# A long convolution whose last transform writes two 64-column tiles of the array in one pass, fed by gathers that write eight partitions each

## The chip, the core and the metric

The kernel runs on one core of a Trainium2 chip. The metric is the time of one execution on the device, in microseconds (us). One program computes a two-layer decoder for two sequences of 2048 positions and 512 channels; the change touches one of its stages.

## What is computed

The stage in question is the sequence mixing of the second layer. Cut to what matters, with u the normalised input, seen as 4 sequences of 1024 positions:

```python
k = einsum('blh,dh->bdl', u, Wk) + bk ;  v = einsum('blh,dh->bdl', u, Wv) + bv
k = irfft(rfft(k_kernel, n=2*L) * rfft(k, n=2*L))[..., :L] + k_D * k      # first convolution
kv = k * v
y = irfft(rfft(kv, n=2*L) * rfft(ssm_kernel, n=2*L))[..., :L] + kv * D     # second convolution
```

Every channel is convolved on its own with a kernel as long as the sequence. The reference sees 2048 positions per batch entry, so a segment of 1024 positions needs its own part and a part from the segment before it.

## The kernel before

**Stages.** `build_decoder` runs attention, cross attention, feed-forward, projection (`stage_project`, which writes `conv_k`, `conv_v`), the convolution (`stage_conv`, lines 2456 to 2806), the gated output, a second cross attention, routing and 64 experts, one after another. `open_conv` (2429) allocates the tables of the convolution and starts their loads during the projection.

**Steps and slots of the convolution.** The 512 channels are done in two halves of 256 (`hh`). For each half and each of the two convolutions (`conv` 0 and 1) there is one step for the kernel's own transform (a *hat* step, `is_seg` false) and four *segment* steps for (batch b, segment s), s = 0 and 1. That makes 20 steps, n = 0 to 19: hats are n = 0, 5, 10, 15; segments with conv 0 are n = 1 to 4 and 11 to 14, with conv 1 n = 6 to 9 and 16 to 19; in each group of four, s is 0, 1, 0, 1. Each step has four slots q = 0 to 3. What TensorE does in slot (n, q) is written out by hand at lines 2798 to 2806: `back` (inverse transform, 32x64 tiles of the array, line 2788) of the slot before, then the slot's auxiliary units, then `spectrum` (forward transform, 64x32 tiles, line 2775) of the next slot. Auxiliary units are, in q = 0 and 1, four *split* units each of step n+1 (line 2753); in q = 2 and 3, two *join* units each of step n-1 if that was a segment (line 2761). All matmuls are float32 with 512 or 256 columns moving; the trace shows each matmul of the program as two records.

**A join unit** multiplies the gathered `vt` with the table `join`: two matmuls of 128 rows by 128 columns of weights, 512 columns moving, the second accumulated on the first, into one of two banks. The result is multiplied on VectorE into `vb` in conv 0 (`take`, line 2723) or copied on ScalarE in conv 1 (line 2647). A bank is free for unit a+2 when unit a was taken.

**The other engines.** ScalarE copies the split units to `g1` (2645), the spectra of hats (2660) and of segments with s = 0 (2667), and the result of `back` to `v1` (2675). VectorE does the complex product of a segment (`point`): with s = 1 two additions (2699, 2700), then four products (2707) and two sums (2711, 2713); `back` waits for the sums.

**Transfers.** `spread` on the SP queue moves `g1` to `gt` (16 DMAs of 128 KB per step, line 2602, 16 source partitions each). `gather` on the POOL queue moves `v1` to `vt` (16 DMAs of 128 KB per segment step, line 2575): 128 source partitions, and 16 destination partitions, every eighth from `PLACE[r]` on, with 8 KB in each. The same SP queue loads `xin` (2586) and `vb` (2592) and stores `y_out` (2607), 1 MB each over 128 partitions. In steps of conv 0 there is mostly one load of `xin` and one of `vb`; in steps of conv 1 one store. SP issues in the order of lines 2609 to 2624; a split unit's copy to `g1` waits until the `spread` of the step before has landed (2644).

## Time and profile before

| | us |
|---|---|
| median of 3 runs | 5086.95 |
| lowest, highest | 5080.97, 5093.71 |
| profiled execution: time, span | 5107.29, 5105.5 |
| convolution stage in that execution (first to last slot) | 484.3, from 2157.7 to 2642.0 |
| mean granted TensorE clock, whole span | 0.978 of full speed |

The span is the time between the first and last instruction; 1.8 us lie around it. Times in rows are microseconds from the start of the span unless they are called ns. PE is TensorE's matmul, PEld its weight load, DVE VectorE, ACT ScalarE, POOL GpSimd, SP the sync engine; "SPq" and "POOLq" are the instructions by which they issue transfers. An entry such as `[2.63 <-DVE cv_y L2713]` says how long the engine had been idle before the row and what ended that. The DMA share is the mean busy share of the core's 16 DMA engines, counted by their packets, and can be a little over 1.

### The profile page before, as it was taken

The page shows a single profiled execution, that of the slowest core. Times are in us where ns is not written, and L with a number is a line of the kernel's source. Part 1 is how long each engine was busy: PE and PEld are TensorE (multiplying, and loading weights), DVE is VectorE, ACT ScalarE, POOL GpSimd, SP SyncE. Part 2 cuts the span into 40 slices and gives each one's busy share as a digit, 9 for nine tenths or more (in the row PEclk, how much of TensorE's full clock was granted, in tenths as well). Part 3 has the DMA queues.
Part 4 walks back from the last instruction along what each step waited for, and adds up shares of the span by engine and source line. Part 5 has one row for each costly group of instructions (what it writes and reads, how often), then busy time and mean ns, then how long its engine had stood idle before and what let it go on. Part 6 is the DMA issues. An engine that isn't in the chain of part 4 may idle for free. (4 is left out here: it accounts for less than half of the span.)

```text
span 5105.5 us, 124764 instructions
## 1 busy us (share of the span) xinstructions
PE 4847.5 (95%) x49200; PEld 3357.9 (66%) x49200; DVE 2858.2 (56%) x4880; ACT 1662.8 (33%) x2033; POOL 1812.5 (36%) x1684
## 2 busy tenths in 40 slices
PE   9999999989999999989979999789999999999998
PEld 4444445658887756534334566478889888888788
DVE  4244236766654345466752576566666666666665
ACT  1001005544333210045431444233333333333333
POOL 1001004645554411022232234444445444444443
PEclk9999999989999999999989999899999999999999
DMA  1000011141111233397866111146666677889996
GB/s 61 9 33 25 9 58 56 59 117 41 41 34 34 75 109 107 119 245 221 216 210 256 49 51 51 50 118 222 222 221 223 222 248 258 306 304 318 312 316 201
DMA packets 422050, 743.99 MB, mean 146 GB/s; under 512 B 119905, under 2 KB 203622, under 8 KB 415284
## 3 DMA queue, kind: packets, MB, share of 16 engines
q1 hardware_dynamic: 293376, 661.44, 36.9%
q0 software_dynamic: 48448, 76.66, 6.7%
q10 hardware_dynamic: 79988, 2.67, 1.0%
q8 instruction: 155, 2.54, 0.2%
q14 instruction: 83, 0.68, 0.0%
HBM read 559.39 MB, written 107.88 MB: 131 GB/s over the span
## 5 line engine op out<-in xcount | busy, mean ns | idle before, releaser
L3562 PE MATMUL ex_ps<-ex_w,ex_xT 128*32 128x256 f32 x20992 | 1228.3, 380 | 31.4 <-DVE ex_w L3463 22.3
L3562 PEld LDWEIGHTS ex_ps<-ex_w,ex_xT 128*32 128x32 f32 x20992 | 1027.9, 110 | 178.1 <-DVE ex_w L3463 30.7
L3463 DVE COPY ex_w<-ex_shelf 128x4096 f32 x328 | 748.8, 2283 | 329.2 <-PE ex_ps L3562 161.2
L3520 ACT ACTIVATE ex_w<-ex_shelf 128x4096 f32 x164 | 595.0, 3628 | 809.5 <-PE ex_ps L3574 687.8
L3574 PE MATMUL ex_ps<-ex_w,ex_hT 128*32 128x256 f32 x10496 | 650.3, 379 | 9.1 <-ACT ex_w L3520 4.1
L3426 POOL DMA_INDIRECT out<-ex_y,ex_ix_out x164 | 306.6, 1869 | 824.4 <-DVE ex_xT L3450 350.4
L3409 POOL DMA_INDIRECT ex_x<-moe_xn,ex_ix x328 | 528.6, 1612 | 137.4 <-issue 99.1
L3574 PEld LDWEIGHTS ex_ps<-ex_w,ex_hT 128*32 128x32 f32 x10496 | 521.9, 110 | 83.8 <-issue 17.9
L2575 POOL DMA_DIRECT2D cv_vt<-cv_v x256 | 134.1, 530 | 376.6 <-ACT cv_v L2675 372.3
L634 PE MATMUL at_ps<-at_xT,at_kT 128*128 128x512 f32 (+3 forms) x640 | 239.3, 529 | 1.6 <-ACT at_kT L528 1.6
L634 PEld LDWEIGHTS at_ps<-at_xT,at_kT 128*128 128x128 f32 x640 | 116.7, 190 | 121.8 <-issue 109.1
L3525 ACT ACTIVATE ex_g<-ex_ps 128x512 f32<-128x512 f32 x164 | 98.2, 599 | 302.5 <-issue 296.6
L3469 DVE TENSOR_TENSOR ex_h<-ex_g,ex_ps 128x512 f32<-128x512 f32 x164 | 112.3, 685 | 132.3 <-PE ex_ps L3562 78.3
L1880 ACT ACTIVATE ff_gT<-ff_ps,ff_bet,ff_gam 128x128 f32<-128x128 f32 x384 | 137.8, 484 | 121.8 <-PE ff_ps L1923 121.8
L1864 ACT ACTIVATE ff_y<-ff_y,ff_nm,ff_rs 128x512 f32<-128x512 f32 x96 | 72.9, 808 | 268.6 <-POOL ff_nm L1580 268.6
L928 POOL TENSOR_TENSOR xb_s<-xb_s,xb_rec 128x616 f32<-128x616 f32 x64 | 78.0, 1219 | 215.4 <-DVE xb_rec L1002 215.1
L3450 DVE STREAM_TRANSPOSE ex_xT<-ex_x 128x256 f32<-128x256 f32 x164 | 72.5, 442 | 139.6 <-DMA ex_x<-moe_xn,ex_ix 139.4
L592 PE MATMUL at_ps<-at_v,at_low 128*128 128x512 f32 x336 | 146.8, 592 | 0.0
L489 DVE TENSOR_TENSOR at_ps<-at_ps,at_tri 128x128 f32<-128x128 f32 x32 | 9.5, 298 | 234.9 <-PE at_ps L634 234.9
L2322 PE MATMUL pr_ps<-pr_t,pr_s 128*128 128x384 f32 x384 | 135.8, 487 | 1.6 <-DVE pr_t L2245 1.1
L2707 DVE TENSOR_TENSOR cv_m<-cv_z,cv_hat 128x512 f32<-128x512 f32 x128 | 79.9, 686 | 99.9 <-ACT cv_z L2667 99.3
L462 DVE TENSOR_TENSOR at_acc<-at_acc,at_ps 128x512 f32<-128x512 f32 x80 | 54.4, 687 | 135.1 <-PE at_ps L592 135.1
(367 smaller groups left out, 8065.9 us busy)
## 6 DMA issues: line engine op xcount, KB each, us to landing
ex_shelf<-L_ffn_w SPq DMA_DIRECT2D x128, 2048.0 KB
ex_shelf<-L_ffn_wo SPq DMA_DIRECT2D x64, 2048.0 KB
cv_gt<-cv_g SPq DMA_DIRECT2D x320, 128.0 KB
cv_vt<-cv_v POOLq DMA_DIRECT2D x256, 128.0 KB, 3.3
ff_x<-x SPq DMA_DIRECT2D x16, 1024.0 KB
ex_raw_x<-slot_token ACTq DMA_DIRECT2D x656, 0.5 KB
at_low<-x SPq DMA_DIRECT2D x8, 1024.0 KB
x<-at_acc SPq DMA_DIRECT2D x8, 1024.0 KB, 4.2
```

The lines of the kernel that those rows point to most:

```text
L592: i = pe.matmul(ps[:, 4 + n % 4, :], prob[g][:, j % 4, (it - 4 * g) * P:(it - 4 * g + 1) * P], v[:, j, :], start=j == js[0], stop=j == js[-1])
L634: i = pe.matmul(ps[:, bank + ic - origin // CH, lo - ic * CH:], kT[:, k, j * P:(j + 1) * P], xT[:, k, lo:(ic + 1) * CH], start=k == 0, sto ...
L1880: i = act.activation(gT[:, k, j * P:(j + 1) * P], ps[:, side_bank(("g", s, j)), k * P:(k + 1) * P], ACT.Gelu, bias=bet[:, b, k:k + 1], sca ...
L2322: i = pe.matmul(bank[:, 0:NPC], lhs[:, k], rhs[:, k], start=first and k == 0, stop=k == HK - 1, skip_group_check=not first)
L2575: eng.dma_start(vt[PLACE[r]:P:UN, e % 2, q // 2], v1[:, q % 2, a, :]).then_inc(vt_in[e % 2][q], 16)
L3409: pool.indirect_dma_start(out=x[:, p, h, :], out_offset=None, in_=xn_q, in_offset=bass.IndirectOffsetOnAxis(ap=ix[:, p, h:h + 1], axis=0)) ...
L3426: pool.indirect_dma_start(out=out_q, out_offset=bass.IndirectOffsetOnAxis(ap=ix_out[:, p:p + 1], axis=0), in_=y[:, p, :], in_offset=None, ...
L3463: dve.tensor_copy(w_s[n][:, :], pick(shelf[n], buf)).then_inc(w_set[n].sem, 1)
L3469: dve.tensor_tensor(h[:, p % 2], g[:, p % 2], ps[:, 1, :], ALU.mult).then_inc(h_done.sem, 1)
L3520: act.activation(w_s[2][:, :], pick(shelf[2], buf), ACT.Copy).then_inc(w_set[2].sem, 1)
L3562: mm = pe.matmul(ps[r * LANES:(r + 1) * LANES, which, hh * FL:(hh + 1) * FL], xT[:, p % 2, k, hh * LANES:(hh + 1) * LANES], wu[which][:, k ...
L3574: mm = pe.matmul(ps[r * LANES:(r + 1) * LANES, 4, 0:DQ], hT[:, p % 2, k, hh, :], wd[:, k, q * DQ:(q + 1) * DQ], start=k == 0, stop=k == FC ...
```

## The change

The join takes one pass in place of two accumulated ones. Each of its two matmuls now has 64 columns of weights, a full contraction over 128 rows, and writes one half of the bank's partitions. For this every gather brings both halves of its rows (`l` = 0 and 1) into the same partitions, so the gathers write 8 partitions (32 a + q + 4 x) with 16 KB in each instead of 16 partitions with 8 KB. The rows of the data are permuted accordingly: loads and the store are split in two DMAs of 64 partitions each, with new counts in their waits. The tables keep their sizes; `join` has only its first 64 columns in use.

```diff
+def base_row(r):
+    return 32 * (r % 4) + r // 4
...
 def half_rows(v, hh, first=0):
     at = hh * (v.shape[0] // (D // CW)) + first
-    return v[at:at + UN * P, :].rearrange("(p i) d -> p i d", i=UN)
+    return v[at:at + UN * P, :].rearrange("(j l k i) d -> l j k (i d)", l=2, k=2, i=UN)
...
     def early(sp):
-        sp.dma_start(st.xin[:, 0], half_rows(kkT, 0)).then_inc(st.x_in[0], 16)
+        for l in range(2):
+            sp.dma_start(st.xin[64 * l:64 * l + 64, 0], half_rows(kkT, 0)[l]).then_inc(st.x_in[0], 16)
...
         def gather(eng, n, q):
             for a in range(4):
-                r = 4 * (q % 2) + a
-                eng.dma_start(vt[PLACE[r]:P:UN, e % 2, q // 2], v1[:, q % 2, a, :]).then_inc(vt_in[e % 2][q], 16)
+                eng.dma_start(vt[base_row(4 * q + a):base_row(4 * q + a) + 29:4, e % 2], v1[:, q % 2, a, :]).then_inc(vt_in[e % 2][q], 16)
...
-                sp.dma_start(xin[:, l % 2], src).then_inc(x_in[l % 2], 16)
+                for k in range(2):
+                    sp.dma_start(xin[64 * k:64 * k + 64, l % 2], src[k]).then_inc(x_in[l % 2], 16)
...
-                sp.dma_start(vb[:, slot_of[n]], seg_rows(v_in, n)).then_inc(v_in_s[slot_of[n]], 16)
+                for k in range(2):
+                    sp.dma_start(vb[64 * k:64 * k + 64, slot_of[n]], seg_rows(v_in, n)[k]).then_inc(v_in_s[slot_of[n]], 16)
...
-                sp.dma_start(seg_rows(y_out, n), vb[:, slot_of[n]]).then_inc(stored[slot_of[n]], 16)
+                for k in range(2):
+                    sp.dma_start(seg_rows(y_out, n)[k], vb[64 * k:64 * k + 64, slot_of[n]]).then_inc(stored[slot_of[n]], 16)
...
-                    for q in range(2):
-                        rows = vt[:, e % 2, q, 2 * u:2 * u + 2, :].rearrange("p i d -> p (i d)")
-                        i = pe.matmul(bank, join[:, q, :], rows, start=q == 0, stop=q == 1)
+                    for l in range(2):
+                        rows = vt[:, e % 2, l, 2 * u:2 * u + 2, :].rearrange("p i d -> p (i d)")
+                        i = pe.matmul(ps[64 * l:64 * l + 64, a % 2, :], join[:, 0, 0:64], rows, start=True, stop=True)
```

## Rows read from the trace of the kernel before

**Rows 1.** Windows: us, each engine's busy time (instructions), clock, DMA share, GB/s; whole stage.

```profile
2157.70:2642.00 484.30, 435.83 (x5184) 181.12 (x5184) 297.96 (x483) 229.07 (x352) 134.08 (x256) 0.95 0.78 214
```

**Rows 2.** Windows: steps 1 to 4, 5, 6 to 9, 11 to 14, 16 to 19.

```profile
2188.90:2288.00 99.10, 88.96 (x1104) 37.39 (x1104) 74.54 (x122) 42.29 (x63) 31.39 (x60) 0.95 0.95 257
2288.00:2307.90 19.90, 19.90 (x193) 7.96 (x192) 4.26 (x7) 9.97 (x17) 2.38 (x5) 1.00 0.75 188
2307.90:2397.70 89.80, 86.74 (x1105) 36.43 (x1104) 69.94 (x114) 49.26 (x74) 31.06 (x60) 0.96 0.75 207
2417.60:2512.20 94.60, 85.89 (x1112) 36.21 (x1114) 74.56 (x122) 42.91 (x64) 31.14 (x60) 0.98 0.90 257
2532.00:2620.00 88.00, 79.86 (x1094) 33.79 (x1094) 69.92 (x113) 45.01 (x67) 31.34 (x60) 0.96 0.65 184
```

**Rows 3.** Groups of the stage: line, tile, shape, count, busy us, mean ns, idle before.

```profile
L2761 PE MATMUL cv_ps<-cv_vt,cv_join 128*128 128x512 f32 x256 | 120.2, 614 | 6.0 <-DMA cv_vt<-cv_v 6.0
...
L2575 POOL DMA_DIRECT2D cv_vt<-cv_v x256 | 134.1, 530 | 376.6 <-ACT cv_v L2675 372.3 <-issue 4.2
```

**Rows 4.** Timeline, PE: a slot with joins in step 7 (start, us, instruction).

```profile
2346.01 1.09 PE L2775 MATMUL cv_ps<-cv_gt,cv_fwd 64*32 64x256 f32 x32
...
2348.09 3.70 PE L2761 MATMUL cv_ps<-cv_vt,cv_join 128*128 128x512 f32 x8
...
2351.72 1.09 PE L2775 MATMUL cv_ps<-cv_gt,cv_fwd 64*32 64x256 f32 x32
```

**Rows 5.** Page, costliest groups: matmuls of the experts on four 32-column tiles.

```profile
L3562 PE MATMUL ex_ps<-ex_w,ex_xT 128*32 128x256 f32 x20992 | 1228.3, 380 | 31.4 <-DVE ex_w L3463 22.3
```

**Rows 6.** Timeline, PE: two slots in a row that VectorE paces, step 19.

```profile
2604.07 2.01 PE L2788 MATMUL cv_ps<-cv_y,cv_inv 32*64 32x256 f32 x32 [2.63 <-DVE cv_y L2713]
...
2609.00 1.12 PE L2788 MATMUL cv_ps<-cv_y,cv_inv 32*64 32x256 f32 x32 [1.22 <-DVE cv_y L2713]
```

**Rows 7.** Timeline, DVE and ACT: join slots of step 2, first slot of step 3; one ACT copy.

```profile
2235.02 1.28 DVE L2723 TENSOR_TENSOR cv_vb<-cv_ps,cv_vb 128x512 f32<-128x512 f32 x2
2236.22 0.68 DVE L2699 TENSOR_TENSOR cv_zp<-cv_ps,cv_z 128x512 f32<-128x512 f32 x1
...
2241.15 1.28 DVE L2723 TENSOR_TENSOR cv_vb<-cv_ps,cv_vb 128x512 f32<-128x512 f32 x2
2242.61 2.50 DVE L2707 TENSOR_TENSOR cv_m<-cv_z,cv_hat 128x512 f32<-128x512 f32 x4 [0.18 <-ACT cv_z L2667]
...
2245.62 0.68 DVE L2713 TENSOR_TENSOR cv_y<-cv_m 128x512 f32<-128x512 f32 x1
...
2352.92 1.08 ACT L2667 ACTIVATE cv_z<-cv_ps 128x512 f32<-128x512 f32 x2 [0.49 <-PE cv_ps L2775]
```

**Rows 8.** Timeline, PE: join slots of hat step 5, and the tail.

```profile
2299.62 3.70 PE L2761 MATMUL cv_ps<-cv_vt,cv_join 128*128 128x512 f32 x8
...
2304.28 3.70 PE L2761 MATMUL cv_ps<-cv_vt,cv_join 128*128 128x512 f32 x8
...
2627.11 9.21 PE L2761 MATMUL cv_ps<-cv_vt,cv_join 128*128 128x512 f32 x16 [6.02 <-DMA cv_vt<-cv_v]
```

**Rows 9.** Windows: feed-forward weights to 128, then to 32 partitions; loads of xin, vb.

```profile
1041.00:1045.00 4.00, 4.00 (x33) 1.93 (x32) 0.64 (x1) 0.73 (x2) 0.00 (x0) 1.00 1.01 372
1045.50:1049.50 4.00, 3.81 (x48) 3.02 (x46) 3.53 (x7) 2.79 (x4) 2.44 (x2) 1.00 1.01 195
2195.00:2199.00 4.00, 3.99 (x39) 1.84 (x40) 2.98 (x5) 3.17 (x5) 1.02 (x2) 1.00 1.05 354
```

**Rows 10.** DMA queues, 2185 to 2630: packets, MB, share of the engines; POOL's queue.

```profile
q0 software_dynamic: 12288, 33.57, 27.6%
```

**Rows 11.** Timeline, SP: the issues of one step's spread.

```profile
2246.88 12.58 SPq L2602 DMA_DIRECT2D cv_gt<-cv_g  x16
```

**Rows 12.** Timeline, PE: the end of a stall in step 2.

```profile
2225.40 3.54 PE L2753 MATMUL cv_ps<-cv_xin,cv_split 128*128 128x512 f32 x4 [3.89 <-ACT cv_g L2645]
```

**Rows 13.** Windows: the stretch of that stall.

```profile
2222.00:2227.00 5.00, 1.60 (x2) 0.84 (x3) 1.68 (x3) 2.00 (x3) 1.55 (x3) 0.82 1.09 246
```

More of the change, by code:

```diff
@@ L2416, in transform_tables @@
     by_row = np.arange(P).reshape(UN, P // UN)[np.argsort(PLACE)].T.reshape(P)
-    split = split.reshape(P, 2, P)[:, :, by_row]
-    join = join.reshape(2, P, P)[:, by_row]
+    halved = np.arange(P).reshape(RES, 2, 2).transpose(1, 0, 2).reshape(P)
+    by_slot = np.array([[base_row(r) + 4 * x for x in range(UN)] for r in range(RES // 2)]).reshape(P)
+    split = split.reshape(P, 2, P)[halved][:, :, by_row]
+    narrow = np.zeros((RES, 2, 2, RES, 2))
+    for k in range(2):
+        narrow[:, :, k, :, k] = join[:, :, 0, :, 0]
+    join = np.zeros((2, P, P))
+    join[0, by_slot, 0:P // 2] = narrow.reshape(P, P // 2)
+    inv = inv.reshape(4, RT, RES // 8, 2, 2, 2, 2, 2, UN).swapaxes(6, 7)
     return (split.reshape(P, 2 * P).astype(f), fwd.reshape(P, RES * RT).astype(f),
@@ L2447, in early @@
         sp.dma_start(st.fwd.rearrange("p a b c -> p (a b c)"), tables_d[1]).then_inc(st.tab_in[1], 16)
-        sp.dma_start(st.xin[:, 1], half_rows(k_in, 0)).then_inc(st.x_in[1], 16)
+        for l in range(2):
+            sp.dma_start(st.xin[64 * l:64 * l + 64, 1], half_rows(k_in, 0)[l]).then_inc(st.x_in[1], 16)
         sp.dma_start(st.inv.rearrange("p a b c d -> p (a b c d)"), tables_d[2]).then_inc(st.tab_in[2], 16)
@@ L2606, in store @@
                 st.plain(sp)
-                sp.dma_start(seg_rows(y_out, n), vb[:, slot_of[n]]).then_inc(stored[slot_of[n]], 16)
+                for k in range(2):
+                    sp.dma_start(seg_rows(y_out, n)[k], vb[64 * k:64 * k + 64, slot_of[n]]).then_inc(stored[slot_of[n]], 16)
             spread(0, 0)
@@ L2623, in _ @@
             for p in range(SEGS):
-                sp.wait_ge(stored[p], 16 * NH)
+                sp.wait_ge(stored[p], 32 * NH)
         @block.gpsimd
@@ L2683, in tap @@
                 l = load_of[n]
-                dve.wait_ge(x_in[l % 2], 16 * (l // 2 + 1))
+                dve.wait_ge(x_in[l % 2], 32 * (l // 2 + 1))
                 dve.tensor_tensor(xin[0:1, l % 2, 0, :], xin[0:1, l % 2, 0, :], gain[0:1, hh, conv, :], ALU.add).then_inc(tapped, 1)
@@ L2720, in take @@
                 if u == 0:
-                    dve.wait_ge(v_in_s[slot_of[n]], 16 * (half_of[n] + 1))
+                    dve.wait_ge(v_in_s[slot_of[n]], 32 * (half_of[n] + 1))
                 o = vb[:, slot_of[n], 2 * u:2 * u + 2, :].rearrange("p i d -> p (i d)")
@@ L2747, in aux @@
                         elif n in load_of:
-                            pe.wait_ge(x_in[load_of[n] % 2], 16 * (load_of[n] // 2 + 1))
+                            pe.wait_ge(x_in[load_of[n] % 2], 32 * (load_of[n] // 2 + 1))
                         else:
@@ L2758, in aux @@
                             pe.wait_ge(vt_in[e % 2][q], 64 * (e // 2 + 1))
-                    for q in range(2):
-                        rows = vt[:, e % 2, q, 2 * u:2 * u + 2, :].rearrange("p i d -> p (i d)")
-                        i = pe.matmul(bank, join[:, q, :], rows, start=q == 0, stop=q == 1)
+                    for l in range(2):
+                        rows = vt[:, e % 2, l, 2 * u:2 * u + 2, :].rearrange("p i d -> p (i d)")
+                        i = pe.matmul(ps[64 * l:64 * l + 64, a % 2, :], join[:, 0, 0:64], rows, start=True, stop=True)
                 i.then_inc(aux_mm, 1)
```

2 lines of the change are left out of this document (1 added, 1 removed).

## The prediction

> **What bounds the kernel now.** Only `stage_conv` changes, so I first cut that stage out of the span: 484 us, in which PE is busy 436, VectorE 298, ScalarE 229 and the DMA engines 0.78 of the time [rows 1]. Then the same view by groups of steps, because the stage has two kinds of them [rows 2]. In steps 6 to 9 and 16 to 19 (conv 1) the DMA share is 0.75 and 0.65 and PE is the busiest. In steps 1 to 4 and 11 to 14 (conv 0) PE leads as well, but the DMA engines stand at 0.95 and 0.90: there a second bound lies right behind the first. Third, the groups by line say how much PE time the change touches: 256 records of the join, 120.2 us [rows 3]. Fourth, the timeline of PE shows a join slot without gaps: from one spectrum to the next 5.71 us, of which the join takes 2351.72 - 2348.09 = 3.63 [rows 4]. So PE sets the pace of a join slot, and I have to find for each slot what comes next.
>
> **What one pass saves on PE.** There are 16 segment steps with two join slots each, 32 slots. The four matmuls of a slot stay four, but two can run side by side. No row shows two tiles of 64 columns. The nearest is the experts' group: four tiles of 32 columns, full contraction, 256 columns moving, 1228.3 us / 20992 = 58.5 ns a record [rows 5]. A join record moves 512 columns in 3.63 / 8 = 454 ns [rows 4], so 227 ns for 256 on one tile: four tiles give 3.9 times the throughput. I take 1.85 for two: 3.63 becomes 1.96, a saving of 1.67 per slot, 53 us over 32. The bounds are 0 (no overlap) and 1.82 (exactly half). Slots already change between tile shapes before and after the join, so that adds nothing: 32x64 before, 64x32 after.
>
> **Who is late next, slot by slot.** Two slots now take 11.42 us, and 3.34 less would be 8.08.
> - Segment with s = 1, conv 1 (steps 7, 9, 17, 19): `back` waits for VectorE's sums. Where nothing else held it, VectorE's pitch was 2609.00 - 2604.07 = 4.93 [rows 6]. Two slots: 9.86, with a hand-over of 0.1 about 10.0, so 1.4 saved. Four times: 5.6.
> - s = 0, conv 1 (8, 18): ScalarE's copy of the spectrum (1.08) and VectorE's 2245.62 + 0.68 - 2242.61 = 3.7 follow each other [rows 7]. The first slot's sums are done 5.0 after its spectrum, the second's 3.8 later, then `back` can start: 9.2, against 11.4 now. 2.2 saved, twice: 4.4.
> - s = 1, conv 0 (2, 4, 12, 14): VectorE also takes the join units. Its pitch is 2241.15 - 2235.02 = 6.13 [rows 7], above today's 5.71; the lag is today made good in the next step. Two sums are ready 11.1 after the first spectrum, `back` starts at 11.4 today: 0.2 saved, so nothing.
> - s = 0, conv 0 (3, 13): 3.7 + 1.2 for the units. 1.2 saved, twice: 2.4.
> - Hats (5, 10, 15): no VectorE work but the units; two joins of 3.63 stand in a row with one spectrum each [rows 8]. 3.3 saved, three times: 10.0.
> - Tail: 9.21 us of joins, the first part at half clock, after a wait of 6.02 for the last gather [rows 8]. I take 3 saved.
>
> This makes 25.4, not 53: half of PE's gain is given back to VectorE. Without the 2.4 in conv 0 it is 23.0.
>
> **What the transfers cost.** Gathers: same bytes, same number of issues; POOL's 256 issues of 530 ns are 134 us of a stage of 484 [rows 3] and hide. With destination partitions of 16 KB the packets can only get easier. Now 33.57 MB take 27.6% of 445 us, 123 us [rows 10]; at the 354 GB/s of the loads [rows 9] it would be 95. So 0 to 28 us less DMA time over 16 steps, 0 to 14 over the eight of conv 0; I take 7. Loads and store: 1 MB over 128 partitions becomes twice 512 KB over 64. The rows show what fewer partitions do: at the same full share the feed-forward weights ran at 372 GB/s to 128 partitions and at 195 to 32 (with some smaller pieces among them) [rows 9]. Half the rate would make a 1 MB load 5.6 us in place of 3.0 (1049 KB / 354), +2.6. Conv 0 has two such loads in each of eight steps: 0 to +42 us of DMA time. Free DMA time there is 0.05 x 99.1 + 0.10 x 94.6 = 14.5 [rows 2]. I take +30 for the loads, nearer to the row than to nothing, since the POOL queue can use an engine while the other waits: 30 - 7 - 14.5 = +8.5 us on the eight steps, which also swallows the 2.4 above. In conv 1 one store per step meets a share of 0.65 to 0.75 and hides. SP issues 16 gathers in 12.58 of some 23 us [rows 11]; two or three more issues of about 0.8 fit. The last store ends the stage: one more issue and at most 2.6 for the halves, +1.5. The first loads of `xin` run during the projection, long before their use.
>
> The Trainium skill (SBUF — State Buffer, "Can I just issue two DMAs to hit both halves?") says that 64 partitions reach no more DMA ports than 32, and that two DMAs on the two halves serialise. The row of 195 against 372 agrees for 32; no row shows 64. By that rule alone the load price would be the full +42.
>
> **Sum.** 23.0 - 1.5 - 8.5 = 13 us less. The profiled execution took 5107.3 and would take 5094.3; that execution is 20 us (0.4%) above the median of the runs, so I put the same 13 us on 5086.95: **5074**.
>
> **The rivals.**
> - *The loads cost nothing* (the two halves interleave, or the gathers' relief pays): conv 0 gives 2.4 and pays nothing, 25.4 - 1.5 = 24: 5063. For it: packets of both queues already share the engines up to 1.09 [rows 13]. Against it: the row at half rate. With relief also ending the stalls, 5057.
> - *Slower: the DMA engines become the bound of conv 0.* Place: steps 1 to 4 and 11 to 14. Price: the full 42 us, no relief, 14.5 absorbed, +27.5. It then meets what happens today once: a copy to `g1` waited for a spread, PE stood 3.89 us [rows 12], and the granted clock averaged 0.82 in the window around it [rows 13], that is, part of it at 1.2 GHz. Two or three more such stalls cost 4 to 8. Total -21.5 + 27.5 + 6 = +12: 5099. It decides from a load price of about 36 us on.
> - *Each gather runs on eight of the 16 engines.* If always the same eight, their gather time doubles, 123 us more over the stage (7.7 a step [rows 10]); conv 0 would then lose some 50 us net: 5110 and more. If they alternate, nothing changes. The Trainium skill (DMA: Bandwidth & Descriptors, on why the semaphore goes up by 16) says that the number of engines divides the outermost dimension of both sides, here 8, and that transfers issued from GpSimd take turns among the engines. No row shows it.
> - *The two tiles don't overlap.* Then the join keeps 3.63 and only the transfers count: 0 to +10, 5087 to 5097. The experts' row speaks against it.
>
> **How the numbers follow.** A measurement of this kernel tells about 0.3%, 15 us, from no change. Forecast (loads partly paid, 5066 to 5084): 0.45. Loads free: 0.32. DMA-bound conv 0: 0.15. Same eight engines: 0.03. No overlap: 0.05. Faster by over 0.3% (below 5071.7): all of "loads free" and a quarter of the forecast, 0.43. Slower by over 0.3% (above 5102): 0.12, from the ends of the second, third and fourth rival. Within: 0.45. The range of 8 in 10 leaves out the better end of "free" and the worse half of the slow ones: 5057 to 5099.
>
> **What would show it.** Join slots: the join's records 128x64, two side by side, some 2.0 us a slot; if 3.6, the first step fails. Pitch of PE in join slots 4.9 to 5.1 with idle time before line 2788 put down to `cv_y`: the VectorE step holds. Hat join slots near 3.0. Steps 6 to 10 and 16 to 19 shorter by about 1.4 to 2.2, hats by 3.3. Steps 1 to 4 and 11 to 14 as long as now or longer, DMA share near 1.0, at fewer GB/s while `xin` and `vb` load: the load price. If these steps get shorter, the price was wrong; if conv 1 gets longer too, it is the gathers. The granted clock of conv 0 falling below 0.95 would be the second rival's mark.

## The result

The changed kernel takes 5143.45 us (median of 4 runs, 5135.74 to 5149.74) against 5086.25 (4 runs, 5080.97 to 5093.71): 1.1% slower, ratio 1.011 with an interval of 1.009 to 1.013, 57 us. The forecast was 13 us less, in a range that ended at 5099. Medians and ratios leave out one slow execution, of e11 below (9285 us at a mean granted clock of 0.82, where the others took some 5093).

The profiled execution of the changed kernel took 5135.74 us (span 5133.9, mean granted clock 0.970). The two profiled executions lie only 28 us apart, because before's was 20 us above its median and after's 8 below. So from here on I compare the stage, cut the same way in every kernel: from the start of the first split matmul to the start of the last join matmul. Before it is 2157.7 to 2635.7, 478.0 us; after 2156.1 to 2682.4, **526.3 us**: 48.3 us longer. The other 9 of the 57 us are not located: each stage is that of one execution. To see where the 48.3 lie, I cut it in four at the first copy to `hat` of steps 0, 5, 10 and 15. Quarters 1 and 3 hold the conv 0 segments, quarters 2 and 4 those of conv 1. Columns are those of [rows 1]. Windows of before at these cuts (not among its rows above):

```profile
2174.20:2289.20 115.00, 102.33 (x1256) 42.59 (x1264) 75.74 (x124) 51.31 (x79) 31.68 (x60) 0.94 0.93 251
2289.20:2398.90 109.70, 106.64 (x1304) 44.38 (x1311) 73.57 (x119) 59.83 (x92) 33.44 (x64) 0.97 0.75 204
2398.90:2513.30 114.40, 105.69 (x1304) 44.12 (x1311) 75.66 (x124) 54.68 (x84) 33.44 (x64) 0.99 0.90 253
2513.30:2635.70 122.40, 108.24 (x1295) 45.46 (x1296) 72.99 (x118) 57.88 (x88) 35.52 (x68) 0.94 0.61 170
```

The same windows of the changed kernel:

```profile
2172.60:2308.70 136.10, 97.44 (x1248) 38.31 (x1248) 73.44 (x120) 51.33 (x80) 34.77 (x59) 0.86 1.00 206
2308.70:2419.30 110.60, 92.57 (x1296) 36.73 (x1296) 74.45 (x122) 58.88 (x92) 37.80 (x65) 0.98 0.88 195
2419.30:2557.30 138.00, 101.89 (x1296) 39.14 (x1296) 74.61 (x122) 54.16 (x85) 37.94 (x65) 0.88 0.99 219
2557.30:2682.40 125.10, 95.25 (x1296) 36.82 (x1296) 75.19 (x122) 57.10 (x88) 41.32 (x70) 0.88 0.75 169
```

The quarters of conv 0 are 21.1 and 23.6 us longer, at a full DMA share that moves fewer bytes a second (206 in place of 251 GB/s). The quarters of conv 1 gain nothing either, though PE is busy 13 to 14 us less in each.

The step on PE came as predicted. Timeline of PE, two join slots of step 7 (answering to [rows 4]) and two of the first conv 0 block:

```profile
2366.34 1.12 PE L2804 MATMUL cv_ps<-cv_y,cv_inv 32*64 32x256 f32 x32 [1.25 <-DVE cv_y L2729]
2367.39 1.94 PE L2777 MATMUL cv_ps<-cv_vt,cv_join 128*64 128x512 f32 x8
2369.26 1.09 PE L2791 MATMUL cv_ps<-cv_gt,cv_fwd 64*32 64x256 f32 x32
2371.28 1.12 PE L2804 MATMUL cv_ps<-cv_y,cv_inv 32*64 32x256 f32 x32 [0.92 <-DVE cv_y L2729]
...
2304.58 1.12 PE L2804 MATMUL cv_ps<-cv_y,cv_inv 32*64 32x256 f32 x32 [1.27 <-DVE cv_y L2729]
...
2310.71 1.12 PE L2804 MATMUL cv_ps<-cv_y,cv_inv 32*64 32x256 f32 x32 [2.12 <-DVE cv_y L2729]
```

The join's eight records take 2369.26 - 2367.39 = 1.87 us where they took 3.63, and `back` then comes at VectorE's pitch, 4.94 and 6.13, just the two numbers taken from [rows 6, 7].

What replaced the gain is a wait for gathers. First the groups of the stage (busy, mean ns, idle before), then ScalarE and PE around 2230 us:

```profile
L2777 PE MATMUL cv_ps<-cv_vt,cv_join 128*64 128x512 f32 x256 | 67.9, 655 | 23.0 <-DMA cv_vt<-cv_v 23.0
L2691 ACT ACTIVATE cv_v<-cv_ps 128x1024 f32<-128x1024 f32 x64 | 65.6, 1024 | 173.6 <-DMA cv_vt<-cv_v 99.1 <-PE cv_ps L2804 74.5
```

```profile
2229.44 1.02 ACT L2691 ACTIVATE cv_v<-cv_ps 128x1024 f32<-128x1024 f32 x1 [8.81 <-DMA cv_vt<-cv_v]
2230.36 1.08 ACT L2661 ACTIVATE cv_g<-cv_ps 128x512 f32<-128x512 f32 x2
```

```profile
2231.01 3.39 PE L2769 MATMUL cv_ps<-cv_xin,cv_split 128*128 128x512 f32 x4 [7.02 <-ACT cv_g L2661]
```

Read them upwards. PE stood 7.02 us before a split, because its bank had not been emptied: that is the work of ScalarE's copy to `g1` at 2230.36. That copy stood behind the copy to `v1` at 2229.44, and this one waited 8.81 us for the gathers out of the `v1` buffer it wanted to overwrite. PE's next four split records then took 3.39 us, mostly at the clock's lower level, 1.2 GHz (mean granted clock 0.58 from 2231.0 to 2234.4); four of the same shape take 1.98 at 2349.03. Before, ScalarE waited for gathers 22.7 us in all (7 times); now 99.1 us (21 times). The DMA view of the stage shows the same, before and then after: the queues with packets, MB and share of the engines, and the gathers' issues with the median us to landing.

```profile
q0 software_dynamic: 12288, 33.57, 25.7%
cv_vt<-cv_v POOLq DMA_DIRECT2D x256, 128.0 KB, 3.3
```

```profile
q1 hardware_dynamic: 50080, 68.18, 59.3%
q0 software_dynamic: 20480, 33.70, 29.6%
cv_vt<-cv_v POOLq DMA_DIRECT2D x256, 128.0 KB, 5.3
```

Where q0 held the engines for 25.7% of 478.0 us, 123 us, it now holds them 29.6% of 526.3, 156 us, for the same data. It has 8192 more packets in the stage, 32 for each of the 256 gathers; only 0.13 MB are in them. POOL needs 600 ns for an issue where it needed 530 [rows 3].

### The profile page after: what moved, and what is told of

Read it like the earlier page. It is cut to its first block and busy times, and to the rows that moved or that the text cites. A ratio compares the mean times of both kernels' runs of the same rounds, so it can differ in the third digit from the quotient of the medians.

```text
span 5133.9 us, 124792 instructions
## 1 busy us (share of the span) xinstructions
PE 4789.1 (93%) x49200; PEld 2841.0 (55%) x49200; DVE 2860.4 (56%) x4880; ACT 1659.7 (32%) x2033; POOL 1851.6 (36%) x1684
## 3 DMA queue, kind: packets, MB, share of 16 engines
q1 hardware_dynamic: 293824, 661.44, 38.1%
## 5 line engine op out<-in xcount | busy, mean ns | idle before, releaser
L3578 PE MATMUL ex_ps<-ex_w,ex_xT 128*32 128x256 f32 x20992 | 1173.9, 381 | 35.9 <-DVE ex_w L3479 32.0
L3578 PEld LDWEIGHTS ex_ps<-ex_w,ex_xT 128*32 128x32 f32 x20992 | 683.4, 110 | 498.6 <-DVE ex_w L3479 47.7
L3590 PE MATMUL ex_ps<-ex_w,ex_hT 128*32 128x256 f32 x10496 | 598.3, 380 | 3.9 <-ACT ex_w L3536 3.9
L3442 POOL DMA_INDIRECT out<-ex_y,ex_ix_out x164 | 318.0, 1939 | 782.3 <-DVE ex_xT L3466 284.2
L3590 PEld LDWEIGHTS ex_ps<-ex_w,ex_hT 128*32 128x32 f32 x10496 | 342.9, 110 | 229.6 <-ACT ex_w L3536 5.1
L2588 POOL DMA_DIRECT2D cv_vt<-cv_v x256 | 151.8, 600 | 408.5 <-ACT cv_v L2691 380.0
L634 PEld LDWEIGHTS at_ps<-at_xT,at_kT 128*128 128x128 f32 x640 | 116.7, 190 | 121.8 <-issue 109.1
L3466 DVE STREAM_TRANSPOSE ex_xT<-ex_x 128x256 f32<-128x256 f32 x164 | 72.7, 443 | 157.9 <-DMA ex_x<-moe_xn,ex_ix 157.9
L2769 PE MATMUL cv_ps<-cv_xin,cv_split 128*128 128x512 f32 x192 | 109.7, 714 | 45.6 <-ACT cv_g L2661 36.1
```

Source lines behind the costliest of these rows:

```text
L634: i = pe.matmul(ps[:, bank + ic - origin // CH, lo - ic * CH:], kT[:, k, j * P:(j + 1) * P], xT[:, k, lo:(ic + 1) * CH], start=k == 0, sto ...
L2588: eng.dma_start(vt[base_row(4 * q + a):base_row(4 * q + a) + 29:4, e % 2], v1[:, q % 2, a, :]).then_inc(vt_in[e % 2][q], 16)
L3442: pool.indirect_dma_start(out=out_q, out_offset=bass.IndirectOffsetOnAxis(ap=ix_out[:, p:p + 1], axis=0), in_=y[:, p, :], in_offset=None, ...
L3578: mm = pe.matmul(ps[r * LANES:(r + 1) * LANES, which, hh * FL:(hh + 1) * FL], xT[:, p % 2, k, hh * LANES:(hh + 1) * LANES], wu[which][:, k ...
L3590: mm = pe.matmul(ps[r * LANES:(r + 1) * LANES, 4, 0:DQ], hT[:, p % 2, k, hh, :], wd[:, k, q * DQ:(q + 1) * DQ], start=k == 0, stop=k == FC ...
```

## Experiments

My theory after the result: the loads and stores in halves slow conv 0, as priced, only more. The rival: the gathers to eight partitions do it. The runs below stand beside their own runs of the kernel before, which there took 5106 to 5114 us; ratios are to those. "Stage" is measured as above in the profiled execution; "gathers land" is the median time in us from the issue of a gather to its landing. A stage is one execution, a ratio is of 4 to 27 on each side. Turned into microseconds, the ratios agree with the stages within 6 us, except for the changed kernel (8) and e15 (13) (and e2, see below). So a difference of less than some 6 us between two rows of the table is not shown, and where the ratios say something else than the stages I give both.

| kernel | stage | quarters 1 to 4 | gathers land | ratio to before (95%) |
|---|---|---|---|---|
| before | 478.0 | 115.0, 109.7, 114.4, 122.3 | 3.3 | |
| changed | 526.3 | 136.1, 110.7, 137.9, 125.1 | 5.3 | 1.0111 (1.0091 to 1.0130) |
| e1_halves_only | 511.7 | 131.3, 108.7, 125.9, 129.2 | 4.3 | 1.0064 (1.0047 to 1.0081) |
| e2_gathers_only | 502.4 | 123.5, 110.5, 125.8, 126.1 | 4.5 | 1.0124, see below |
| e3_tiles_only | 459.4 | 111.5, 102.1, 114.8, 115.0 | 3.4 | 0.9970 (0.9958 to 0.9983) |
| e4_whole_loads | 491.4 | 120.0, 109.6, 124.0, 121.8 | 5.5 | 1.0020 (1.0008 to 1.0032) |
| e5_gather_order | 525.2 | 132.4, 110.2, 136.9, 129.4 | 5.3 | 1.0098 (1.0080 to 1.0117) |
| e6_eight_far_apart | 603.7 | 145.3, 136.5, 157.9, 148.1 | 8.1 | 1.0246 (1.0227 to 1.0266) |
| e7_sixteen_in_half | 468.3 | 115.7, 105.6, 113.2, 119.0 | 4.0 | 0.9972 (0.9963 to 0.9982) |
| e8_every_other | 477.9 | 111.9, 109.6, 115.2, 124.7 | 3.2 | 1.0000 (0.9989 to 1.0011) |
| e9_v1_three | 467.4 | 108.7, 107.5, 114.3, 120.8 | 6.6 | 0.9984 (0.9975 to 0.9994) |
| e10_v1_three_before | 470.9 | 108.9, 110.2, 110.5, 124.7 | 3.3 | 0.9974 (0.9965 to 0.9983) |
| e11_v1_three_ordered | 459.2 | 106.1, 104.2, 112.8, 120.2 | 5.2 | 0.9969 (0.9960 to 0.9979) |
| e12_after_v1_three | 505.6 | 120.9, 111.0, 126.2, 130.9 | 6.6 | 1.0057 (1.0044 to 1.0071) |
| e13_two_queues | 516.9 | 129.0, 111.6, 129.3, 128.9 | 5.8 | 1.0086 (1.0071 to 1.0101) |
| e14_pool_loads | 710.3 | 198.0, 139.1, 190.3, 154.1 | 5.0 | 1.0465 (1.0451 to 1.0479) |
| e15_store_halves | 466.3 | 105.0, 111.6, 110.9, 122.8 | 5.4 | 1.0003 (0.9993 to 1.0012) |

### One part at a time

**e1_halves_only**: the kernel before, with its loads and its store in two DMAs each.

```diff
-                sp.dma_start(xin[:, l % 2], src).then_inc(x_in[l % 2], 16)
+                for k in range(2):
+                    sp.dma_start(xin[64 * k:64 * k + 64, l % 2], src[64 * k:64 * k + 64]).then_inc(x_in[l % 2], 16)
```

> The kernel before with one part of the change: every load of xin and vb and every store of y goes out as two DMAs of 64 partitions. Gathers and join as before. Theory L (the halves are what made the change slow): in the trace of the changed kernel DMA time per packet of these transfers doubles, about 46 us more DMA time in the stage; two thirds fall into the eight steps of conv 0, which had 14.5 us free, so 15 to 25 us slower than before (5101 to 5111), with the losses in steps 1 to 4 and 11 to 14 and the DMA share there near 1.0. Theory G (the gathers to eight partitions are what made it slow): within 5 us of before, since the halves only fill free DMA time.

**e2_gathers_only**: the kernel before, with the gathers of the changed one.

```diff
-                eng.dma_start(vt[PLACE[r]:P:UN, e % 2, q // 2], v1[:, q % 2, a, :]).then_inc(vt_in[e % 2][q], 16)
+                eng.dma_start(vt[base_row(4 * q + a):base_row(4 * q + a) + 29:4, e % 2], v1[:, q % 2, a, :]).then_inc(vt_in[e % 2][q], 16)
```

> The kernel before with one other part alone: each gather of vt writes 8 partitions with 16 KB in each instead of 16 with 8 KB; loads, store and join matmuls as before, so the join reads its rows in the wrong places and the output is not the reference's. Theory L: within 8 us of before, landing time of a gather near 3.3 us as before. Theory G: 25 to 40 us slower than before (5111 to 5126), landing time of a gather near 5.3 us as in the changed kernel, and ScalarE waiting for cv_vt before it writes cv_v (99 us in the changed kernel, 22.7 before).

**e3_tiles_only**: the kernel before, with the join on two column tiles and nothing else.

```diff
-                        i = pe.matmul(bank, join[:, q, :], rows, start=q == 0, stop=q == 1)
+                        i = pe.matmul(ps[64 * q:64 * q + 64, a % 2, :], join[:, q, 0:64], rows, start=True, stop=True)
```

> The kernel before with only the join changed: its two matmuls have 64 columns of weights each and write two halves of the bank's partitions, with no accumulation; half of the join's products are left out, so the output is not the reference's. Transfers as before. Both theories: the slot sum of the prediction, 25 us faster than before (5061, range 5056 to 5068): join slots 4.9 to 5.3 us with s = 1 and conv 1, hats 3.0. A third theory, that the transfers of before already stand in the way of a faster PE: 5 to 15 us faster only, with new waits for cv_gt or cv_vt.

**e4_whole_loads**: the changed kernel, with whole loads and stores.

```diff
-    return v[at:at + UN * P, :].rearrange("(j l k i) d -> l j k (i d)", l=2, k=2, i=UN)
+    return v[at:at + UN * P, :].rearrange("(p i) d -> p i d", i=UN)
...
-                for k in range(2):
-                    sp.dma_start(xin[64 * k:64 * k + 64, l % 2], src[k]).then_inc(x_in[l % 2], 16)
+                sp.dma_start(xin[:, l % 2], src).then_inc(x_in[l % 2], 16)
```

> The changed kernel with only the loads of xin and vb and the store put back to one DMA of 128 partitions each, in natural order of the rows, so that the rows stand in other partitions than the tables want and the output is not the reference's. Tiled join and gathers to eight partitions stay. Theory L: most of the loss goes, 5060 to 5080, DMA share of conv 0 below 1.0. Theory G: 5115 to 5135, landing time of a gather still near 5 us.

Measured: halves +33.7 alone (511.7 - 478.0) and +34.9 in the changed kernel (526.3 - 491.4). Gathers +24.4 alone, and +32.0 where the join is fast (491.4 - 459.4). Tiles -18.6. Put in one after another (tiles, gathers, halves), the parts make -18.6 + 32.0 + 34.9 = 48.3; that is the stage's whole difference by construction. Each alone beside the kernel before they make -18.6 + 24.4 + 33.7 = 39.5, so some 9 us come only when they meet. Both theories held, each with about half of the loss, and each had expected the other's part to be near nothing; the halves cost more than the 15 to 25 that theory L gave them. The tiles gained less than the 25 expected, with a longer wait of PE for spreads (11.3 us in place of 5.9), as the third theory had it.

The two parts don't act by separate paths. In e1 the gathers are those of before, and yet they land after 4.3 us and ScalarE waits 39.0 us for them in place of 22.7: the halves load the DMA engines, and part of their price goes by the same ring of `v1`.

In e2 the whole kernel lost 63 us, of which only 24 lie in this stage. Its rows are mixed up in the join, other tokens go to other experts, and the experts' first product has 21504 records in place of the 20992 of [rows 5]:

```profile
L3566 PE MATMUL ex_ps<-ex_w,ex_xT 128*32 128x256 f32 x21504 | 1260.1, 380 | 28.4 <-DVE ex_w L3467 20.1 <-ACT ex_g L3529 3.5 <-issue 2.1
```

In e1, e3, e4, e6 to e9, e11 and e15 it is 20992. Since e2's whole time says little of the change, the stage is what I compare throughout.

The quarters tell who pays where. Halves (changed less e4): +16.1 and +13.9 in conv 0, +1.1 and +3.3 in conv 1. Gathers (e4 less e3): 8.5, 7.5, 9.2, 6.8, much the same everywhere, though conv 1 has free DMA time: that looks like a latency, not like a lack of bandwidth. Tiles (e3 less before): -3.5, -7.6, +0.4, -7.3.

### What makes a half expensive

**e8_every_other**: e1 again, but each DMA takes every other partition.

```diff
-                    sp.dma_start(xin[64 * k:64 * k + 64, l % 2], src[64 * k:64 * k + 64]).then_inc(x_in[l % 2], 16)
+                    sp.dma_start(xin[k:P:2, l % 2], src[k:P:2]).then_inc(x_in[l % 2], 16)
```

> The kernel before with every load of xin and vb and every store in two DMAs of 64 partitions, as in e1_halves_only (stage 511.7 against 478.0, ratio 1.0064), but the even and the odd partitions in place of the lower and the upper 64. Reach theory (one half of the partitions can only be reached at half the rate): the price is gone, stage 476 to 484, ratio to before 0.999 to 1.002. Count theory (what costs is 64 partitions to a DMA, two issues, two semaphore counts): stage 505 to 515, ratio 1.005 to 1.008.

The stage is 477.9, before's to a tenth, and the ratio 1.0000. So neither the second issue, nor 64 partitions, nor 512 KB cost anything that shows; only which partitions. (e8 is the kernel before; the tiled join with loads and stores split like this was not run.) The 16 us from the first of four load DMAs on, windows of e1, of e8, and of before with its two:

```profile
2195.00:2211.00 16.00, 11.86 (x204) 4.84 (x202) 12.41 (x21) 9.34 (x15) 4.51 (x8) 1.00 1.03 224
```

```profile
2192.30:2208.30 16.00, 11.96 (x212) 5.04 (x218) 12.41 (x21) 9.81 (x16) 4.51 (x8) 1.00 1.01 286
```

```profile
2192.30:2208.30 16.00, 11.64 (x204) 4.84 (x202) 12.41 (x21) 9.12 (x15) 4.52 (x8) 0.99 1.02 277
```

At the same full share the lower-and-upper halves move 224 GB/s, the interleaved ones 286. The Trainium skill (SBUF — State Buffer, "Door 1: The DMA port swizzle") says that bits 4 to 2 and bit 6 of a partition's number choose its port, so a half has 8 of 16 and every other partition all 16; e1 against e8 agrees.

**e15_store_halves**: e11 (below), with the store alone in halves.

> As e11_v1_three_ordered (whole loads and stores, v1 three deep, ordered gathers; rows in another order than the reference's; stage 459.2), with the store alone in two halves. The prediction put the store at +1.5 us in all, the last one's exposure, since conv 1 has free DMA time. If so, stage 459 to 463, and the 46 us between e11 and e12 belong to the loads of conv 0. Rival: the stores cost conv 1 half of it, stage 475 to 485.

+7.1 on the stage against e11 (466.3 to 459.2), between the two expectations, and by quarters -1.1, +7.4, -1.9, +2.6: it is conv 1 that pays, where I had 1.5 for the last store and nothing for the others. Here the whole times say more than the stage: e15's ratio is 1.0003 and e11's 0.9969, some 17 us, and e15's profiled execution (5100.48) is among the fastest of its ten (median 5111.18). So the stores cost 7 to 17 us. The rest of the 46 between e11 and e12, 29 to 39, is put down to the loads by subtraction; no run has the loads alone in halves.

**e13_two_queues**: e12 (below), with each upper half issued by ScalarE.

```diff
-                        load_x(load_of[n + 1] + 2)
+                        load_x(sp, load_of[n + 1] + 2, 0)
...
+                    if q == 2 and n + 1 in load_of and load_of[n + 1] + 2 < len(loaded):
+                        load_x(act, load_of[n + 1] + 2, 1)
```

> As e12_after_v1_three (the changed kernel with its loads and stores in halves, v1 three deep, gathers in the order 0, 2, 1, 3; stage 505.6 us, ratio 1.0057), with the upper half of every load and store of the stage issued by ScalarE in place of SyncE, at the same places of the order. The output is that of the reference. The theory of reach says that a transfer to 64 partitions holds one half of the ways and leaves the other idle; e11_v1_three_ordered, with whole transfers, had a stage of 459.2. Two readings of it. Halves in one queue stand behind each other and only that costs: with the halves in two queues the engines can take a packet of one and a packet of the other in turn, both halves are reached, and the stage falls to 462 to 478, ratio 0.997 to 1.000, faster than the kernel before. Or the ways are given out per transfer and two transfers don't add up, whatever their queues: stage 500 to 512, ratio 1.005 to 1.008.

516.9 against 505.6: worse, in quarters 1 and 3. It doesn't settle the question. The two halves of `xin` were issued 7 to 14 us apart, and those of `vb` mostly 3 to 7; ScalarE issued its first one of `vb` at 2186.9, SyncE, behind its spreads, at 2191.1. And the spreads came late: PE waited 38.1 us for them (15.5 in e12), ScalarE 24.9 (0.5), which may hide a gain.

```profile
L2603 ACTq DMA_DIRECT2D cv_vb<-conv_v x8: 514/514/1472, 2186.9 to 2518.5; - x8
L2603 SPq DMA_DIRECT2D cv_vb<-conv_v x8: 536/808/1804, 2191.1 to 2518.3; - x8
```

### What makes a gather to eight partitions expensive

**e5_gather_order**: the changed kernel, with neighbouring gathers in different halves.

```diff
-            for a in range(4):
+            for a in (0, 2, 1, 3):
```

> The changed kernel with the four gathers of a group issued in the order 0, 2, 1, 3. Gather a writes eight partitions four apart from 32a on, so in the natural order two gathers that follow each other 0.6 us apart write into the same half of the partitions (0-31 and 32-63, then 64-95 and 96-127); in this order neighbours write into different halves. Reach theory (a gather is slow because it and its neighbour need the same way into the same half): the landing median falls from 5.3 us to about 4, the stage from 526 to 500 to 515 us, the kernel is 10 to 25 us faster than the changed one (ratio to before 1.006 to 1.009). Count theory (what costs is that only eight partitions, so perhaps eight engines, carry each gather, whatever the place): within 4 us of the changed kernel, ratio to before 1.010 to 1.012, landing median unchanged.

The stage stays (525.2), the landing median stays (5.3), and yet the DMA share falls from 0.90 to 0.85: 474 us of DMA time become 446. Summed more finely over the queues it is 472 and 448: a saving of some 24 us of the engines' time that is worth 1 us of the stage (the two ratios, 1.0098 and 1.0111, overlap). The stage was not waiting for just that throughput.

```profile
2154.60:2679.80 525.20, 403.98 (x5182) 157.27 (x5184) 297.60 (x483) 227.08 (x351) 151.28 (x256) 0.88 0.85 196
```

```profile
2156.10:2682.40 526.30, 399.54 (x5184) 155.62 (x5184) 297.68 (x483) 226.25 (x351) 151.83 (x256) 0.89 0.90 195
```

**e7_sixteen_in_half**: e3, with each gather to sixteen partitions of one half.

```diff
-                eng.dma_start(vt[PLACE[r]:P:UN, e % 2, q // 2], v1[:, q % 2, a, :]).then_inc(vt_in[e % 2][q], 16)
+                at = 64 * (a // 2) + 2 * (q % 2) + a % 2
+                eng.dma_start(vt[at:at + 61:4, e % 2, q // 2], v1[:, q % 2, a, :]).then_inc(vt_in[e % 2][q], 16)
```

> The kernel before with the tiled join and whole loads as in e3_tiles_only (stage 459.4; half of the products are left out and the contents of the join are permuted, so the output differs), and each gather still to 16 partitions, but 4 apart within one half of the partitions instead of 8 apart over the whole height; two neighbours in the same half, then two in the other. Count theory (16 on the narrow side is what kept gathers cheap): stage 457 to 463, landing median 3.3 to 3.6. Reach theory: the stage rises to 475 to 492 and the landing median to 4.5 to 5.5, as with eight partitions.

+8.9 on the stage (459.4 to 468.3), landing 4.0: between the two expectations. But the ratios of e3 and e7 are the same (0.9970 and 0.9972), and e7's profiled execution is 5 us above its median, so keeping sixteen partitions and two neighbours within one half costs 0 to 9 us. The other 23 to 32 of the gathers' 32 come with going from sixteen partitions of 8 KB to eight of 16 KB.

**e6_eight_far_apart**: e4, with the eight partitions 16 apart.

```diff
-    return 32 * (r % 4) + r // 4
+    return r
...
-                eng.dma_start(vt[base_row(4 * q + a):base_row(4 * q + a) + 29:4, e % 2], v1[:, q % 2, a, :]).then_inc(vt_in[e % 2][q], 16)
+                eng.dma_start(vt[base_row(4 * q + a):base_row(4 * q + a) + 113:16, e % 2], v1[:, q % 2, a, :]).then_inc(vt_in[e % 2][q], 16)
```

> Whole loads and stores (as in e4_whole_loads, whose stage took 491.4 us, with rows in another order, so the output differs), and the eight partitions of each gather 16 apart over the whole height instead of 4 apart within 32; the join table follows. Count theory: nothing changes, stage 488 to 495, landing median 5.5. Reach theory in its simple form (spreading over the whole height is what helps): the stage falls to 465 to 475 and the landing median to about 3.5 to 4. A third outcome, that the stage gets longer than 500: then it is neither height nor count, but how many different groups of partitions with a way of their own a gather meets, and 16 apart meets fewer of them than 4 apart.

The third outcome, far more than I had thought: 603.7, 112 us worse than e4, landing 8.1. The gathers' queue holds the engines 41.5% of 603.7 us, 251 us, where e4's holds them 30.2% of 491.4, 148:

```profile
q0 software_dynamic: 20480, 33.70, 41.5%
```

So spreading over the height is not what helps; eight partitions 4 apart, as the change has them, are the better choice. By the rule of the Trainium skill above (SBUF — State Buffer, "Door 1: The DMA port swizzle"), 4 apart meets eight ports and 16 apart four, and the trace agrees in direction, with a factor of 1.7 in the gathers' DMA time.

### Latency or throughput

**e9_v1_three**: e4, with a third buffer of `v1`.

```diff
-        v1 = st.sb("v1", [P, 2, 4, CW])
+        v1 = st.sb("v1", [P, 3, 4, CW])
...
-                        if h >= 2:
-                            pe_, pq = (h - 2) // 4, (h - 2) % 4
+                        if h >= 3:
+                            pe_, pq = (h - 3) // 4, (h - 3) % 4
```

> As e4_whole_loads (changed kernel with whole loads and stores, stage 491.4 us, ScalarE waited 87 us for gathers before its copies to v1), with v1 three buffers deep in place of two, so that a copy to v1 waits for the gathers of three groups back. Latency theory (gathers to eight partitions cost the stage because each lands later, 5.5 us against 3.4 from issue, and the copy to the next v1 buffer waits for that, with the split units queued behind it on ScalarE): the wait falls below 40 us and the stage to 462 to 475. Throughput theory (the DMA engines take 47 us more for the same bytes and are what the stage waits for, wherever the buffers are): stage 486 to 493, and the wait moves to the join's wait for vt or to g1's wait for spreads.

**e10_v1_three_before**: the same edit on the kernel before.

> The kernel before (stage 478.0) with v1 three deep. Here gathers land in 3.3 us and ScalarE waited 22.7 us for them. Both theories: stage 474 to 479, ratio to before 0.998 to 1.001. If it gains more than 6 us, the kernel before already paid for the gathers' latency, and the third buffer must be counted apart from the change.

**e11_v1_three_ordered**: e9, with the order 0, 2, 1, 3 of e5.

> As e9_v1_three, with the four gathers of a group issued in the order 0, 2, 1, 3, so that neighbours write to different halves of the partitions. In e5_gather_order that order took 24 us off the DMA engines' time but only 1 off the stage. Latency theory: with the third buffer little is left to gain, within 4 us of e9_v1_three. Throughput theory: the DMA time taken off now shows, 5 to 12 us under e9_v1_three.

**e12_after_v1_three**: the changed kernel itself, halves and all, with both edits.

> The changed kernel itself, with its loads and stores in halves (stage 526.3, ratio 1.0111), with v1 three deep and the gathers in the order 0, 2, 1, 3; the output is that of the reference. Latency theory for the gathers, reach for the halves: the gathers' 32 us come back in part where conv 0 is not DMA-bound (20 of 32), the halves' 35 stay: stage 502 to 512, ratio to before 1.005 to 1.009. Throughput theory: stage 515 to 526, ratio 1.008 to 1.012.

The third buffer takes 24.0 us off e4 (491.4 to 467.4), although the gathers land later still (6.6) and the engines' time doesn't fall: their share of the stage is 0.92, 430 us, against 0.86, 423. ScalarE's wait for gathers, 87.2 us in 23 times, the longest 7.4, is all but gone (first e4, then e9):

```profile
ACT cv_v L2686 <- DMA cv_vt<-cv_v: 87.2, 23, 7.4
```

```profile
ACT cv_v L2686 <- DMA cv_vt<-cv_v: 2.4, 1, 2.4
```

So a good part of what the gathers cost goes by latency, through a ring of two buffers. The kernel before gains from the third buffer too, 7.1 (13 by its ratio), more than the 6 from which I had said it must be counted apart: so 24.0 - 7.1, some 17 of the gathers' 32 us, are shown to be the price of the ring (11 if 13 is taken off), and for the rest that is not shown. The latency theory had little left for the order of the gathers, and with three buffers it gave 8.2 more (459.2), as the throughput theory said: the share was 0.92, near its end, and now is 0.84. It seems that each theory held where the other's limit had been moved out of the way. Against e10, tiles and gathers together are worth 11.7 us of the stage (470.9 to 459.2), but hardly anything of the whole time: the ratios 0.9974 and 0.9969 overlap and are 3 us apart.

The halves stay. e12, at 505.6 where the latency theory had it (502 to 512), lies 46.4 above e11, and the wait went on to the join, whose wait for gathers is 51.3 us against 22.8 in e11:

```profile
PE cv_ps L2777 <- DMA cv_vt<-cv_v: 51.3, 11, 9.6
```

### Whole transfers with the right rows

e4, e9, e11 and e15 (and e6) load rows in the natural order, which the tiled join doesn't want; e3 and e7 leave half of its products out. To have the changed kernel's output with whole transfers, e14 walks memory as 4 x 32 blocks.

**e14_pool_loads**: e12, with each load and store one DMA over 128 partitions, issued by GpSimd.

```diff
-    return v[at:at + UN * P, :].rearrange("(j l k i) d -> l j k (i d)", l=2, k=2, i=UN)
+    return v[at:at + UN * P, :].rearrange("(j m i) d -> m j (i d)", m=4, i=UN)
...
+                pool.dma_start(vb[:, slot_of[n]], seg_rows(v_in, n)).then_inc(v_in_s[slot_of[n]], 16)
```

> The changed kernel with v1 three deep and the gathers in the order 0, 2, 1, 3 (as e12_after_v1_three, stage 505.6), in which every load and store of the stage is one transfer of all 128 partitions with 8 KB rows, issued by GpSimd among its gathers; in memory the transfer walks the row blocks as 4 x 32, and the tables are permuted to match, so the output is that of the reference. SyncE issues only the spreads. Theory of reach: a transfer over the whole height costs nothing extra, stage 459 to 472 as e11_v1_three_ordered (459.2), ratio 0.997 to 1.000, faster than the kernel before. Rival: with 4 as the outermost count in memory only a few of the 16 engines carry each such transfer, it lands after 10 us and more, and gathers queued behind it on the same engines land late: stage 480 to 500.  A second rival: GpSimd waits for the join before a store and for the split before a load, and the gathers behind these waits come late: the wait would show before the gathers' issues on POOL.

The rival, only worse: 710.3 us. In quarter 1 the share is lower and so is the rate (0.81 and 138 GB/s, the first window below; 0.93 and 251 before), a store takes 20.5 us to land (5.3 before), and a gather up to 30.5 (median 5.0), so that PE waits 165 us for gathers:

```profile
2187.40:2385.40 198.00, 103.10 (x1248) 38.92 (x1248) 75.83 (x123) 51.61 (x80) 41.41 (x69) 0.75 0.81 138
```

```profile
conv_y<-cv_vb POOLq DMA_DIRECT2D x7, 1024.0 KB, 20.5
```

The Trainium skill (DMA: Bandwidth & Descriptors, on why the semaphore goes up by 16) says that the number of engines is the largest up to 16 that divides the outermost count on both sides, here 4. The trace does not name engines; 1 MB in 20.5 us, 51 GB/s, speaks for few of them, but e14 also moved the issues to GpSimd, and the two are not taken apart. The second rival explains little. GpSimd waited 87.3 us before three loads, but 82.4 of them before the stage's first gather at 2212.6, and 24.3 before one store at 2560.4, 20 us ahead of the next gather. Before the gathers themselves it waited 436.7 us for ScalarE's copies to `v1` and 16.8 for nothing that the profile shows, some of it the issues ahead of them.

**The version to use** is e10: the kernel before with a third buffer of `v1`, one line of size and four of indices and waits. It beats both kernels, ratio 0.9974 with an interval of 0.9965 to 0.9983 to the one before, some 13 us. No version with the tiled join and the right rows beat it, and e11, which has the loads whole but in the wrong order, is not clear of it in whole time either.

## Why the prediction was wrong

**The join on PE: right.** 1.96 a slot predicted, 1.87 measured; the pitch of 4.93 and 6.13 taken from VectorE came out as 4.94 and 6.13. The rival without overlap is out.

**What of it reaches the stage: the slots right, the sum a third too large.** 25.4 us of 53 were to be left by VectorE, and 18.6 were measured (e3). Slot by slot, from the start of one spectrum to the start of the next in the traces of before and e3, the terms came out almost as written: a hat 3.5 (3.3), steps 8 and 18 2.4 (2.2), steps 7 and 17 1.2 (1.4), steps 4 and 12 nothing (nothing), the tail's joins 6.25 us in place of 9.21, so 3.0 (3). In the changed kernel too, one hat join follows the other after 2.90 us where it was 4.66 [rows 8]:

```profile
2322.45 1.94 PE L2777 MATMUL cv_ps<-cv_vt,cv_join 128*64 128x512 f32 x8 [1.12 <-DMA cv_vt<-cv_v]
2324.32 1.09 PE L2791 MATMUL cv_ps<-cv_gt,cv_fwd 64*32 64x256 f32 x32
2325.35 1.94 PE L2777 MATMUL cv_ps<-cv_vt,cv_join 128*64 128x512 f32 x8
```

What I had left out are stalls that a faster PE runs into or out of. Most of the missing 6.8 us lies in the second block of conv 0. In e3 PE waits 6.45 us there for a spread, and in step 13 it stands before a split and then runs at the lower clock, 4.0 us more than before for that slot:

```profile
2427.93 1.96 PE L2775 MATMUL cv_ps<-cv_gt,cv_fwd 64*32 64x256 f32 x32 [6.45 <-DMA cv_gt<-cv_g]
...
2465.87 3.22 PE L2753 MATMUL cv_ps<-cv_xin,cv_split 128*128 128x512 f32 x4 [3.04 <-ACT cv_g L2645]
```

A stall of before at the same place in step 12, 3.68 us and the lower clock behind it, is absent from e3 and gives 5.3 back. At the end of this block, in the first slot of step 15, PE runs at the lower clock for a while in e3 and not before: some 1.6. Together these make about 6.8, as much as was missing; smaller differences in other slots roughly cancel.

**The gathers: the sign was wrong.** "With destination partitions of 16 KB the packets can only get easier", I wrote, and took -7. Measured: +24.4 alone, +32.0 beside the fast join. The step that failed is the bound. It had no end above nothing, though no row showed a transfer to eight partitions, and it looked at bytes and at packets' length alone. The rival with eight engines went by throughput too ("if they alternate, nothing changes"). What e9 shows beside e10 is that a gather's *time to landing* has a price of its own: from `v1`'s two buffers a late gather holds ScalarE, and ScalarE's queue holds PE. That path was in the code (`cv_v` waits for `vt_in` two groups back) and in the profile, where ScalarE waited 22.7 us for gathers, 7 times; I had not costed it. What remains unproven is why eight partitions land later: 600 ns of issue in place of 530, 32 more packets, and perhaps half the engines for each gather come together, and I have not taken them apart.

**The halves: right in kind, half the size.** The row of 195 against 372 GB/s [rows 9] pointed the right way, and "half the rate" was in the text with its full price. Without the gathers' relief of 7, which is another term, the forecast had 30 - 14.5 = 15.5 for the loads and 1.5 for the stores, 17.0 in all; e1 measured 33.7. Two steps were mis-sized. I chose 30 of 42, and took off 14.5 us of free DMA time, as if a burst could be moved into gaps elsewhere in a step. The DMA time of e1 is 0.83 x 511.7 - 0.78 x 478.0 = 52 us more, so about two thirds of each added microsecond reached the stage. And the stores, which I had hidden in conv 1, cost 7 to 17 (e15). (The 12.58 us of [rows 11] are the issues of a spread, not of gathers as the forecast says; nothing hangs on it.)

**The slower rival was right on the halves.** It named the place (steps 1 to 4 and 11 to 14) and the mechanism (the DMA engines as bound, stalls of 4 us and more, part of them at 1.2 GHz), and its price of 27.5 + 6 = 33.5 is near what e1 and e4 measured, 33.7 and 34.9. That is in part luck, since it had all of it in conv 0: there the changed kernel has 30.0 more than e4 and e1 27.8 more than before, and the rest is in conv 1. I gave it 0.15, against a row that bore it out, because I held that the other queue could use an engine while the first waits: no row showed that, and e13, which tried two queues, showed nothing of it. Even this rival ended at 5099 because the gathers, in it too, cost nothing.

**The sign that was to tell the cases apart did so only in part**: "if conv 1 gets longer too, it is the gathers". Quarter 2 got 1.0 longer and quarter 4 2.8, where 8.3 and 11.3 were to be gained, and the gathers cost 7.5 and 6.8 there (e4 less e3). But the halves alone lengthened quarter 4 too, by 6.9 (e1), so a longer conv 1 did not point at the gathers alone.

## What to carry to other kernels

Before a transfer is reshaped, look for who waits for its landing through a short ring of buffers, and count what stands in that engine's queue behind the wait: the price of a transfer can be its latency there, and not its share of the bandwidth. Split a transfer over interleaved partitions and not over the lower and the upper half (every other partition cost nothing, the halves 34 us), but don't take height alone for a guide (eight partitions 16 apart cost 112 us more than eight 4 apart), and bound a shape that no row shows from both sides. Where a transfer lands late, one more buffer is a cheap experiment that helps to tell latency from throughput; run it on the kernel before as well, which may gain too. And when a stage is read from one execution, hold it against the whole times of the others before a difference of a few microseconds is believed.

## What the runs showed of the hardware

- 16 us with loads of 64 partitions each in the lower and the upper half: 224 GB/s with a DMA share of 1.03 (e1); in even and odd partitions 286 GB/s at 1.01 (e8).
- A gather of 128 KB took at least 2.2 us to land on 16 partitions 8 apart (before) and 2.7 on 8 partitions 4 apart (e4); on 8 partitions 16 apart (e6) the median was 8.1 us in place of 5.5 and the gathers' DMA time 1.7 times as long.
- Two tiles of 128x64 run side by side at nearly twice the rate of one (1.94 times): eight records of 512 columns in 1.87 us, against 3.63 one after the other.
- A store of 1 MB from GpSimd with 4 as its outermost count in memory took 20.5 us to land (median, e14); from SyncE over 128 partitions 5.3 (before).
- Some 24 us less DMA time changed the stage by 1 us with two buffers and the loads in halves (e5), while 42 to 44 us less went with 8 us with three and whole loads (e11 against e9).
